# CIN kernel: layers 2 and 3 of the first chunk in full f32, its x as a DRAM image, and its picks in four row groups

## The reference, cut to what matters

```python
x0 = sparse_embed                                  # (batch 512, 32 fields, 16 dims), f32
x = x0
for (W, b), split in ((W1, b1, True), (W2, b2, True), (W3, b3, False)):
    h = x.shape[1]                                 # 32, then 64, then 64
    z = einsum('bhd,bmd->bhmd', x, x0).reshape(B, h * 32, D)
    xk = relu(einsum('oc,bcd->bod', W, z) + b)     # 128 outputs
    if split: x, xk = xk[:, :64], xk[:, 64:]       # first half feeds the next layer
    results.append(xk)
y = sum(concat(results, axis=1), axis=2) @ Wo.T + bo
```

## Time and profile before

| | |
|---|---|
| median of three runs | 467.1 us (466.95, 467.1, 467.76) |
| the profiled execution's own time | 466.92 us |
| its span in the profile | 465.0 us, 6018 instructions |
| busy: PE, PEld | 454.0 us (98%), 304.6 us (66%) |
| busy: DVE, ACT, POOL | 420.6 us (90%), 318.7 us (69%), 413.5 us (89%) |
| DMA | 75.66 MB, mean 163 GB/s |

### The profile page before, as it was taken

How to read it: one execution, slowest core, us unless ns; L and a number is a source line. 1 busy time by engine, 2 the same in 40 slices (tenths; PEclk the granted TensorE clock), 3 DMA queues, 4 the chain that set the end, 5 groups by cost and what they waited for, 6 DMA issues and landing times.

```text
span 465.0 us, 6018 instructions
## 1 busy us (share of the span) xinstructions
PE 454.0 (98%) x1620; PEld 304.6 (66%) x1620; DVE 420.6 (90%) x486; ACT 318.7 (69%) x398; POOL 413.5 (89%) x152
## 2 busy tenths in 40 slices
PE   8998699999999999999999999999999999999997
PEld 3355366766767676776767677776767767677774
DVE  0495888999999999999999999999999999999997
ACT  2584766867768586876858687676868768677661
POOL 0458597999989899898999989898999999899995
PEclk9999999999999999999999999999999999999999
DMA  8899987998977949596894959689595953822100
GB/s 203 226 231 222 216 180 165 213 233 178 219 158 170 234 102 226 120 227 140 178 228 107 230 114 224 137 188 218 122 233 106 228 125 86 186 45 47 28 17 1
DMA packets 22784, 75.66 MB, mean 163 GB/s; under 512 B 5843, under 2 KB 5843, under 8 KB 18548
## 3 DMA queue, kind: packets, MB, share of 16 engines
q1 hardware_dynamic: 22772, 75.52, 74.3%
HBM read 59.51 MB, written 0.00 MB: 128 GB/s over the span
## 4 chain that ended last, share of the span: by engine, by line
PE 81%; POOL 7%; DMA 4%; DVE 3%; ACT 3%; SPq 1%; issue 1%; DVEq 0%; POOLq 0%
PE y_ps L826 25%; PE y_ps L832 15%; PE y_ps L814 14%; PE y_ps L816 14%; PE y_ps L822 7%; POOL zl L589 7%; PE y_ps L838 3%; DMA a_rep<-x_sb 2%; DVE z L632 2%; DMA shifted<-xt_dram 1%; PE y_ps L791 1%; ACT zh L493 1%; PE y_ps L818 1%; PE y_ps L834 1%; PE zx_ps L758 0%
## 5 line engine op out<-in xcount | busy, mean ns | idle before, releaser
L589 POOL TENSOR_TENSOR zl<-z,zh 128x1024 fp32r<-128x1024 f32 (+1 forms) x141 | 403.9, 2899 | 33.2 <-ACT zh L493 33.0
L632 DVE TENSOR_TENSOR z<-a_ps,b_fac 128x512 f32<-128x512 f32 (+2 forms) x256 | 271.9, 1085 | 27.0 <-PE y_ps L838 12.3
L493 ACT ACTIVATE zh<-z 128x1024 fp32r<-128x1024 f32 (+1 forms) x141 | 176.2, 1251 | 115.3 <-DVE z L632 115.0
L832 PE MATMUL y_ps<-zl,w_high 128*128 128x512 f32 x330 | 152.5, 555 | 3.2 <-POOL zl L589 3.2
L814 PE MATMUL y_ps<-zh,w_high 128*128 128x512 f32 x330 | 130.5, 396 | 3.9 <-ACT zh L493 3.9
L816 PE MATMUL y_ps<-zh,w_low 128*128 128x512 f32 x330 | 129.1, 391 | 0.0
L826 PE MATMUL y_ps<-z,w_raw 128*128 128x512 f32 x252 | 128.4, 591 | 0.0
L832 PEld LDWEIGHTS y_ps<-zl,w_high 128*128 128x128 f32 x330 | 61.6, 188 | 72.1 <-issue 59.4
L814 PEld LDWEIGHTS y_ps<-zh,w_high 128*128 128x128 f32 x330 | 61.9, 188 | 19.1 <-issue 3.1
L816 PEld LDWEIGHTS y_ps<-zh,w_low 128*128 128x128 f32 x330 | 62.1, 188 | 13.9 <-issue 0.2
L826 PEld LDWEIGHTS y_ps<-z,w_raw 128*128 128x128 f32 x252 | 47.3, 188 | 10.4
(11 more groups left out here) (54 smaller groups left out, 192.3 us busy)
## 6 DMA issues: line engine op xcount, KB each, us to landing
b_fac<-xt_dram SPq DMA_DIRECT2D x52, 512.0 KB, 8.7
shifted<-xt_dram SPq DMA_DIRECT2D x64, 256.0 KB, 4.9
a_rep<-x_sb SPq DMA_DIRECT2D x91, 128.0 KB, 2.4
shifted<-xt_dram SPq DMA_DIRECT2D x64, 128.0 KB, 5.2
b_fac<-xt_dram SPq DMA_DIRECT2D x16, 256.0 KB, 10.1
a_rep<-x_sb SPq DMA_DIRECT2D x62, 64.0 KB, 2.1
w_raw<-w_dram SPq DMA_DIRECT2D x2, 640.0 KB, 5.9
w_raw<-w_dram SPq DMA_DIRECT2D x2, 384.0 KB, 6.7
```

The source lines that it names most:

```text
L493: nc.scalar.activation(zh[:, slot, 0:end - native, :], z[:, slot, native:end, :], ACT.Copy).then_inc(zh_ready, 1)
L589: nc.gpsimd.tensor_tensor(zl[:, slot, 0:end - native, :], z[:, slot, native:end, :], zh[:, slot, 0:end - native, :].bitcast(F32), ALU.subtract
L632: return nc.vector.tensor_tensor(dst, factor.unsqueeze(1).to_broadcast(list(dst.shape)), others, ALU.mult)
L832: mm = nc.tensor.matmul(y, wh[layer][:, w, :], zl[:, slot, t, :], start=False, stop=end_here)
```

## The change

- Groups q0 to q4 and q6 to q9 are native, so all of layers 2 and 3 of chunk 0; their waits for rounded weights move to the first split group of each layer, in iterations 2 and 3 (`splits_before` keeps the counts).
- Chunk 0's x comes from a prepared DRAM array `x0` of 128 rows, as four loads of whole 128-partition tiles in order of use (`XREP`, tiles 0 and 1, tiles 2 and 3, the fifth), with the parts of W1 between them and a semaphore for each.
- Each pick uses its own 32 rows of `shifted` and of the pick matrix (r = 0 to 3), where all used rows 0 to 31.
- `first_a` writes the first layer's outputs straight from PSUM into `a_ps`, ahead of `x_to_sbuf`.
- The second sum of W1 moves from POOL to DVE; the rounding of W2 moves on ACT behind the work of q0's outputs; POOL splits both parts of W3 before the first `zl`.
- SP issues the spread of layer 2 of chunk 0 after the first half of chunk 1's `b_fac` instead of after both.

```diff
-NATIVE_GROUPS = 3
+NATIVE = (0, 1, 2, 3, 4, 6, 7, 8, 9)
...
+            def load_x0(first, end, loaded):
+                sp.dma_start(shifted[:, first * CH:end * CH], x0[:, first * CH:end * CH]).then_inc(loaded, 16)
-            load_ends(0, 0, 0, fields_loaded)
+            load_x0(XREP, XT, fields_loaded)
             sp.dma_start(pick_sb, pick).then_inc(pick_loaded, 16)
-            load_x(0)
+            load_x0(0, NATIVE_CUT, x0_loaded[0])
             sp.dma_start(w1_sb[:, 0:2 * NAT1], w1[:, 0:2 * NAT1]).then_inc(w1_loaded, 16)
+            load_x0(NATIVE_CUT, GT, x0_loaded[1])
             sp.dma_start(w1_sb[:, 2 * NAT1:], w1[:, 2 * NAT1:]).then_inc(w1_rest_loaded, 16)
+            load_x0(XQ, XREP, x0_loaded[2])
...
             load_b_half(1, 0)
+            spread(2, 0, (1,))
             load_b_half(1, 1)
-            spread(2, 0, (1,))
...
+            def first_a():
+                act.wait_ge(group_used, 1)
+                act.wait_ge(cols_loaded, 16)
+                for to in (0, HALF):
+                    copy = nc.scalar.activation(a_ps[to:to + HALF, 0, :], y_ps[1][X_HALF[1], :], ACT.Relu,
+                                                bias=cols_sb[X_HALF[1], 0:1])
+                copy.then_inc(a_in_psum[2][0], 1)
...
+                            first_a()
                             x_to_sbuf(1, 0)
-                            a_to_psum(2, 0, 0)
                             b_from_psum(1)
...
-                for j in range(GT * half, GT * half + GT):
+                for r in range(GT):
                     if half:
-                        pe.wait_ge(b0_made, j - GT + 1)
-                    nc.tensor.matmul(pick_banks[j % GT], pick_sb[:, j, :], shifted[0:Q, XREP * CH:(XREP + 1) * CH],
+                        pe.wait_ge(b0_made, r + 1)
+                    rows = slice(Q * r, Q * r + Q)
+                    nc.tensor.matmul(pick_banks[r], pick_sb[rows, half, :], shifted[rows, XREP * CH:XT * CH],
                                      start=True, stop=True).then_inc(b0_picked, 1)
```

More of the change, by code:

```diff
@@ L126, in dve_tiles_before @@
 def dve_tiles_before(i):
-    if isinstance(i, int) and (i < 2 or i > NCHUNK):
+    if isinstance(i, int) and (i < 3 or i > NCHUNK):
         return sum(by_dve for k in range(i) for *_, by_dve in dve_tiles(k))
-    return i * DVE_PER_ITER + (sum(by_dve for k in range(2) for *_, by_dve in dve_tiles(k)) - 2 * DVE_PER_ITER)
+    return i * DVE_PER_ITER + (sum(by_dve for k in range(3) for *_, by_dve in dve_tiles(k)) - 3 * DVE_PER_ITER)
 def dve_tiles(i):
@@ L149, in is_native, with splits_before, natives_before @@
 def is_native(q):
-    return isinstance(q, int) and q < NATIVE_GROUPS
+    return isinstance(q, int) and q in NATIVE
+def splits_before(q):
+    return q - natives_before(q)
+def natives_before(q):
+    return sum(n < q for n in NATIVE) if isinstance(q, int) else len(NATIVE)
 def i_is(i, number):
@@ L195, in iterate, with cin_kernel @@
         body(i)
-def cin_kernel(nc, xt, pick, w1, w2, w3, cols, bo, out):
+def cin_kernel(nc, xt, x0, pick, w1, w2, w3, cols, bo, out):
     with ExitStack() as ctx:
@@ L322, in load_x, with load_ends @@
                 place = (c % XSLOTS) * (XT * CH)
-                loaded = x0_loaded if i_is(c, 0) else x_loaded
                 for r in range(P // Q):
                     sp.dma_start(shifted[Q * r:Q * r + Q, bass.ds(place, GT * CH)],
[L326 to L330, removed]
+                                 rows_of(c, GT * r, [[CH, Q]], [[1, GT * CH]])).then_inc(x_loaded, 16)
+                    load_ends(c, r, place)
+            def load_ends(c, r, place):
                 ends = shifted[Q * r:Q * r + Q, bass.ds(place + XQ * CH, 2 * CH)].rearrange("p (t n) -> p t n", t=2)
-                sp.dma_start(ends, rows_of(c, Q // 2, [[CH, Q]], [[Q // 2 * CH, 2], [1, CH]])).then_inc(loaded, 16)
+                sp.dma_start(ends, rows_of(c, Q // 2, [[CH, Q]], [[Q // 2 * CH, 2], [1, CH]])).then_inc(x_loaded, 16)
             def load_b(c, parts=None):
@@ L782, in body @@
                         else:
-                            pe.wait_ge(w_loaded[layer][0], 16)
+                            pe.wait_ge(w_loaded[layer][g // 2], 16)
                         pe.wait_ge(z_native_ready, q + 1)
@@ L790, in body @@
                             weights = w_raw[layer][:, (natives + splits).index((g, t)), :]
-                            mm = nc.tensor.matmul(y, weights, z[:, slot, t, :], start=(g == 0 and t == 0), stop=False)
+                            mm = nc.tensor.matmul(y, weights, z[:, slot, t, :], start=(g == 0 and t == 0),
+                                                  stop=(layer > 1 and g == GROUPS[layer] - 1 and t == GT - 1))
                         if layer == 1:
@@ L800, in body @@
                         pe.wait_ge(wq_made, 1)
-                    if layer == 2 and i_is(i, 1) and g == 2:
+                    if layer == 2 and i_is(i, 2) and g == 0:
                         pe.wait_ge(w_split[2], 2)
-                    if layer == 3 and i_is(i, 2) and g in (0, 2):
-                        pe.wait_ge(w_split[3], g // 2 + 1)
+                    if layer == 3 and i_is(i, 3) and g == 0:
+                        pe.wait_ge(w_split[3], 2)
                     by_pool = end - native - QUARTER[layer]
@@ L884 @@
     Wo = np.asarray(L0_rec_Wo)[0]
+    row, block = np.arange(Q)[None, :], np.arange(4)[:, None]
+    shifts = [4 * block + t + row for t in range(4)] + [row + Q // 2 + 0 * block, row + 0 * block]
+    pick = np.repeat(np.eye(Q, dtype=x.dtype).reshape(Q, 4, 8).transpose(0, 2, 1), Q, axis=2)
     arrays = {
         "xt": np.concatenate([x, x], axis=1),
-        "pick": np.repeat(np.eye(Q, dtype=x.dtype).reshape(Q, 4, 8).transpose(0, 2, 1), Q, axis=2),
+        "x0": np.stack([x[0, s.ravel() % Q] for s in shifts], axis=1).reshape(P, -1),
+        "pick": pick.reshape(Q, 2, 4, P).transpose(2, 0, 1, 3).reshape(P, 2, P),
         "w1": np.concatenate([w1a[:, :NAT1], w1b[:, :NAT1], w1a[:, NAT1:], w1b[:, NAT1:], w1q], axis=1),
```

33 lines of the change are left out of this document (18 added, 15 removed).

## The result

The changed kernel takes **463.2 us** (median of six runs, 461.44 to 465.22) against 467.45 for the kernel before on the same chip (six runs, 466.95 to 468.52): a ratio of 0.992, with an interval of 0.9901 to 0.9938, 0.8% faster. The forecast was 462.3, the range 459.5 to 466.3. The profiled execution took 461.44 us with a span of 459.4, 5.6 less than the span of before.

The account below looks back on a forecast made before the run. PE bounds the long loop, transfers the first 60 us. PE gains 8.3 us at q10, cut to 4.7 by DVE, ACT and POOL and rounded to 4.6; from 466.92 that gives 462.3 us, range 459.5 to 466.3.

Parts of the forecast that it names:

- the second spread behind eight loads: Before q10: layer 1 of chunk 1's spread waits behind eight b_fac loads, 9.7 us, landing at 48.5 instead of 53.17.
- q0 near 9.4: Start: picks overlap in part, five pass times instead of eight, 4.3 us, so q0 starts at 9.4.
- W3 near 18.8: SP's queue: after second picks of 2.15 us, W3 is issued near 18.75 instead of 23.13, 4.4 earlier.
- W3 before 16: SP's queue: W3 issued before 16, with q10 near 50, would show that all picks ran at once.
- second case: Rival at the start: all picks at once, q0 from 7 to 14, 2.1 us below forecast, 460.2; chance 0.30.
- the gain at q10: PE starts q10 near 52.0 instead of 60.28, 8.3 us earlier.
- what was given back: Behind q10: DVE's lead shrinks from 6.0 to 2.3 us, so late split tiles cut the 8.3 us gain to 4.7.
- other end 7: Start: at 200 GB/s instead of 390, x tiles 0 and 1 land at 7 instead of near 5.3.
- x of chunk 1 is through by 19 ..., so W3's issue sets the start.: SP's queue: 3.3 MB at 390 GB/s, then 1.5 MB at 200, finish by 19; W3's issue then times later transfers.
- Paid for: First 60 us: six native groups cost PE 0.51 us more each, 3.1 us, covered by removed waits on ACT and POOL.
- 8.3 to 4.7: Behind q10: of 8.3 us gained there, 4.7 remain if DVE, ACT and POOL set the pace.
- The lower clock through the second picks: Slower rival: PE stays at the lower clock, second picks in turn, W3 issued 4.6 us later, 471.5; chance 0.04.

Follow-up runs that it names:

- e1: The changed kernel again with no edit, on another chip: 460.95 us, ratio 0.9879 against the kernel before.
- e4: The changed kernel with all picks back on the first 32 rows: 461.69 us, ratio 0.9886 against the kernel before.
- e7: The changed kernel with x of chunk 1 also loaded as a DRAM image, in eight pieces: 458.9 us, ratio 0.984 against the kernel before.
- e5: The changed kernel with only q0 to q2 native, W2 and W3 roundings and splits in old places: 465.91 us, ratio 0.9985 against the kernel before.
- e11: The changed kernel with layer 3 of chunk 0 (q6 to q9) split again, layer 2 native: 465.68 us, ratio 0.9977 against the kernel before.
- e12: The changed kernel with q6 to q8 split again and q9 native: 463.86 us, ratio 0.9925 against the kernel before.
- e9: e8 with SP's order changed, four b_fac loads ahead of the first spread, four behind the second: 456.77 us, ratio 0.9788 against the kernel before.
- e3: The changed kernel with six f32 matmuls, results overwritten, on PE in the wait before q10: 463.34 us, ratio 0.9919 against the kernel before.
- e8: The changed kernel with x of every chunk from 1 on as a DRAM image, two loads each: 459.06 us, ratio 0.9835 against the kernel before.
- e6: The changed kernel with chunk 0's x loaded by 32 partitions again, picks waiting for all of it: 463.14 us, ratio 0.9927 against the kernel before.

## Why the prediction was right, and where not

The time, the sign and the range were right, and so was the bound named for q10, the second spread behind eight loads. The way there was right only in part: of the signs named for the forecast, q0 near 9.4 and W3 near 18.8 did not come (8.27 and 15.73), and W3 before 16 was named as a sign of the second case, whose time was 460.2. That the time fits better than its terms is partly luck: the gain at q10 was 6.8 instead of 8.3, what was given back 1.2 instead of 3.6, and the two errors offset. Beside each step what was measured:

| step | forecast | measured |
|---|---|---|
| picks end | 9.4 (second case 7) | 6.28 |
| first tiles of x land | 5.3 (other end 7) | 6.55 |
| q0 | 9.4 to 16.4 | 8.27 to 14.4 |
| W3 issued | 18.75 | 15.73 |
| x of chunk 1 landed | 19 | 22.4 |
| first, second spread landed | 37.7, 48.5 | 38.26, 49.60 |
| DVE's product for q10, q10 on PE | 49.65, 52.0 | 50.84, 53.30 |
| time given back behind q10 | 3.6 | 1.2 |
| change of the profiled execution | -4.6 | -5.5 (medians -4.2, in e1 -5.7) |

- **The picks: the second case, without its price.** All four ran at once. The 2.1 us that the case gave for it did not come, since W3's earlier issue gained the queue nothing (e4).
- **The step that failed: "x of chunk 1 is through by 19 ..., so W3's issue sets the start."** It landed at 22.4, and SP stood in `load_x(2)` until then. The amount was nearly right: 3.3 MB, what was ahead of it, had moved by 11.8 us, where 390 GB/s from 2 us on make 10.5, and 4.96 of the 4.98 MB by 19.2. What failed is the order: the forecast put W3 behind that x, but W3, issued at 15.73, shared the queue with it, and 0.7 MB of W3 had moved when x was through. The rows of before could not show this, since W3 was issued there into an empty queue (0 GB/s at 22.5 to 24). With W3 earlier still (14.09, e1) that x landed later, and with W3 late (18.73, e4) earlier; W3's early issue bought nothing.
- **Luck again behind it.** By the forecast the loads of x of chunk 2 were to be issued from 19.7 on (0.94 behind W3, as before); they came from 22.47 on, 2.8 late. But with most of W3 already through they took 10.0 us from the first issue to the landing, not 12.2, and landed at 32.5 against 31.9, so the spreads came out nearly right. e7 takes the wait away and gains 2.55 us at q10.
- **"Paid for" was too little for the native groups.** The forecast put their 3.1 us on PE against waits of the same size and the gain on the queue alone. But the queue's gain reaches PE only if q9 needs nothing of ACT while ACT stands at the second spread. With q9 split, the two spreads come early and the ratio is 0.9985 and 0.9977 (e5, e11); with q9 native it is 0.9925 (e12). I had ACT's order in hand (second spread's copy, then x, then the roundings) and followed it for q10 only.
- **The second spread: right to 1.1 us**, 0.6 of it a later issue. Its price is the loads ahead: 8.86 us behind eight, 2.37 behind none (e9).
- **Given back: the size too large, and in the change itself by another way.** The term was "8.3 to 4.7"; measured from q10's start to chunk 4 it is 46.96 us against 45.74 before, 1.2 given back. In the change q10's slow matmuls, 1.6 us longer, are all of it, and PE waits for nothing more up to 105 us. Where q10 runs at the full clock, POOL is late, as forecast, but with one wait of about 1 us (e3, e7, e8: 1.05, 1.05, 1.08), not with a string of them.
- **The lower clock through the second picks** did not happen: their passes are 0.5 us apart from 14.45 on, and the weight loads had fallen to 0.19 at 12.21.

## What to carry to other kernels

When a start-up is bound by transfers, list for each in-order engine what stands behind its longest wait, and let the work that PE can do meanwhile need nothing of that engine: one group without ACT's rounding was worth some 2.4 us here (e12), faster picks nothing that the runs can tell (e4), an earlier load of chunk 0 between nothing and 2 us (e6). Where a queue runs empty and then full, look for the wait in its issuer's program that holds back loads which were free to go. Ask too who waits for a load that is still under way when the next is issued: with W3 issued earlier, the x ahead of it landed later (e1 beside e4). An order that helps one transfer in a full queue moves the wait to the next; make the loads shorter first.

## What the runs showed of the hardware that was not expected

- Four f32 matmuls of 32 rows, each in rows and a bank of its own, start within 0.02 us and take 1.15 us together with both passes each at granted clock 1.00, against 3.70 in turn (e4).
- Loads that one engine issues to one queue do not wait for one another's end: 0.7 MB of W3, issued at 15.73, had moved before the last load of x of chunk 1, issued at 9.85, landed at 22.4.
- Loads by 128 partitions did not reach their later rate in the first microseconds: per slice of 1.5 us, the changed kernel moved 186, 314, 229 and 381 GB/s from 1.5 to 7.5 us, and 345 to 414 from there to 12. The form of the loads is not the reason by itself: in e8 the queue moves 371 to 408 GB/s from 18 to 24 us, with x of chunk 2 in the same form among the loads.
- One spread of the same size took 8.84 us behind eight loads of 256 KB and 2.37 with none ahead (e8, e9).
